# Two deformable-sampling layers: padded image through DRAM, third window buffer, second patch-sum bank, columns made on TensorE, filler matmuls between the layers

## The reference

```python
# layer 0: 4 sampled points per pixel, softmax weights, 1x1 projection, batch norm, gelu
offsets = conv2d(bev, offset_w, offset_b)              # 3x3, 8 channels out
attn = softmax(conv2d(bev, weight_w, weight_b), axis=1) # 3x3, 4 channels out
sampled = grid_sample_border(bev, gx, gy)              # bilinear, 4 corners per point
aggregated = einsum('bkhwd,bkhw->bdhw', sampled, attn)
y = conv2d(aggregated, proj_w); y = batchnorm(y); return gelu(y)

# layer 1: deformable 3x3 convolution, 9 sampled points per pixel, sigmoid gates
offset = conv2d(x, w_p, b_p); m = sigmoid(conv2d(x, w_m, b_m))
x_off = g_lt*x[lt] + g_rb*x[rb] + g_lb*x[lb] + g_rt*x[rt]   # bilinear
return conv2d(x_off * m, w_conv, stride=3)
```

## Time and profile before

| | us |
|---|---|
| three runs | 570.9, 572.35, 576.16 (median 572.35) |
| profiled execution, its own time | 566.8 |
| span of the profile, first to last instruction | 564.9 |
| TensorE busy (matmul) | 471.1 (83%) |
| VectorE busy | 391.0 (69%) |
| ScalarE busy | 147.2 (26%) |
| GpSimd busy | 345.4 (61%), of it 320 gathers 331.8 |
| mean granted clock of TensorE | 0.905 of full |

### The profile page before, as it was taken

One profiled execution on the slowest core, in us unless ns is written; L12 is line 12 of the kernel. 1 busy time (PEld: TensorE's weight loads), 2 busy tenths in 40 slices (PEclk: granted clock), 3 DMA queues, 4 the chain that ended last, 5 costly groups with the idle time before them and its releaser, 6 DMA issues.

```text
span 564.9 us, 10597 instructions
## 1 busy us (share of the span) xinstructions
PE 471.1 (83%) x3808; PEld 261.8 (46%) x3808; DVE 391.0 (69%) x874; ACT 147.2 (26%) x290; POOL 345.4 (61%) x335
## 2 busy tenths in 40 slices
PE   6679648879695480899999999899999999998894
PEld 3345335555453440354555555355544544543443
DVE  1627527587764650788898797798888788787671
ACT  2311111021102460234333433332332232332201
POOL 4317716754700005677777777777777777777771
PEclk9655878998989585899999999999999999999987
DMA  4379964566850089812232233821212212211211
GB/s 108 114 212 200 207 162 99 122 126 115 153 110 4 19 236 155 185 47 70 74 91 70 69 86 91 108 57 54 59 49 57 56 55 57 57 52 51 57 52 27
DMA packets 50148, 53.28 MB, mean 94 GB/s; under 512 B 24990, under 2 KB 41622, under 8 KB 50096
## 3 DMA queue, kind: packets, MB, share of 16 engines
q1 hardware_dynamic: 39712, 31.28, 26.7%
q0 software_dynamic: 10240, 20.99, 14.0%
q10 hardware_dynamic: 144, 0.30, 0.2%
HBM read 35.85 MB, written 8.72 MB: 79 GB/s over the span
## 4 chain that ended last, share of the span: by engine, by line
PE 35%; POOL 22%; issue 15%; DMA 11%; SPq 7%; DVE 6%; ACT 1%; POOLq 1%; DVEq 0%; ACTq 0%
POOL got L599 22%; SPq L456 5%; PE ps_x L1009 5%; PE ps_pair L1144 4%; PE ps_later L1144 4%; PE ps_x L1157 3%; DMA shared<-positions 3%; PE ps_raw L944 3%; DMA got<-table,idx 2%; PE ps_raw L1120 2%; DMA xn<-xq 2%; DMA columns_of<-table 2%; PE ps_x L1167 2%; DVE samples L1766 2%; PE ps_pair L1019 1%
## 5 line engine op out<-in xcount | busy, mean ns | idle before, releaser
L599 POOL DMA_INDIRECT got<-table,idx x320 | 331.8, 1037 | 137.5 <-issue 95.5
L1766 DVE TENSOR_TENSOR samples<-shared,vprod 128x800 f32<-128x800 f32 x48 | 47.2, 986 | 32.0 <-PE ps_x L1009 20.3
L1009 PE MATMUL ps_x<-early,samples 128*128 128x128 f32 (+1 forms) x336 | 49.3, 296 | 23.8 <-ACT ysumT L705 14.9
L1584 DVE TENSOR_TENSOR vprod<-ps_pair,rhat 128x704 f32<-128x704 f32 x64 | 56.7, 886 | 17.0 <-PE ps_pair L1144 16.5
L1783 DVE TENSOR_TENSOR prod<-got,wgt 128x512 f32<-128x512 f32 x64 | 44.2, 690 | 33.3 <-DMA got<-table,idx 33.1
L1009 PEld LDWEIGHTS ps_x<-early,samples 128*128 128x128 f32 (+1 forms) x336 | 39.3, 145 | 44.9 <-ACT ysumT L705 21.1
L1584 DVE TENSOR_TENSOR vprod<-ps_later,rhat 128x704 f32<-128x704 f32 x64 | 56.3, 880 | 0.2 <-PE ps_later L1144 0.2
L1157 PE MATMUL ps_x<-early,vprod 128*128 128x128 f32 x384 | 55.6, 281 | 0.6 <-DVE vprod L1592 0.4
L1157 PEld LDWEIGHTS ps_x<-early,vprod 128*128 128x128 f32 x384 | 41.9, 143 | 29.8 <-issue 19.4
L1592 DVE TENSOR_TENSOR vprod<-vprod 128x640 f32<-128x640 f32 x64 | 52.7, 824 | 1.2
L1167 PE MATMUL ps_x<-early,prod 128*128 128x128 f32 x256 | 39.3, 276 | 9.3 <-DVE prod L1783 9.1
(11 more groups left out here) (202 smaller groups left out, 657.1 us busy)
## 6 DMA issues: line engine op xcount, KB each, us to landing
shared<-positions SPq DMA_DIRECT2D x24, 440.0 KB, 7.9
got<-table,idx POOLq DMA_INDIRECT x320, 5.4
xn<-xq SPq DMA_DIRECT2D x28, 132.0 KB, 3.0
xn<-xq SPq DMA_DIRECT2D x28, 131.9 KB, 3.1
table<-trow SPq DMA_DIRECT2D x3, 702.0 KB
table<-trow SPq DMA_DIRECT2D x9, 234.0 KB
table<-trow SPq DMA_DIRECT2D x2, 1024.0 KB, 5.5
columns_of<-table SPq DMA_DIRECT2D x4, 512.0 KB, 8.9
```

The source lines that it names most:

```text
L599: pool.indirect_dma_start(into[t][:, s * P:(s + 1) * P], None, tab, bass.IndirectOffsetOnAxis(ap=idx[:, slot, k:k + 1], axis=0),).then_inc ...
L1009: last = nc.tensor.matmul(window_bank[0:m, t * P:(t + 1) * P], wprod[t % 2][:, a:a + m], idn[:], start=(q == 0), stop=(q == len(cuts) - 1) ...
L1584: nc.vector.tensor_tensor(dst, ps_dense[pair_number(0, t, pair) % 2][:].rearrange("p (d n) -> p d n", d=2)[:, :, 0:WROWS * C].rearrange("p ...
L1766: nc.vector.tensor_tensor(wprod[t % 2].rearrange("p (y x c) -> p y x c", y=SIDE, c=C), window[n // TT % 2][:, :, 2 * t * C:(2 * t + SIDE) ...
```

## The change

- **The padded image goes through DRAM.** A normalised image is written once to `image` (DRAM, 68 rows of 66 a channel), and `xn` is loaded from there, two transfers a quarter in place of four. The borders of `image` are zeroed by eight small transfers at the start, so the memset of `xn[:, 1]` goes, and that of `xn[:, 0]` covers eleven rows only. The heads are eleven rows for the lower shifts, and a convolution waits for fewer quarters.
- **Order of the start.** Four input transfers in place of eight; TensorE's filler matmuls at the start (4 and 1) go; image 0 is normalised before its heads; the statistics of image 1 are combined ahead of the last two corner chunks; SyncE's queue has corners and pixels of image 0 ahead of its quarters 2 and 3, and three windows ahead of image 1.
- **Three window buffers** in place of two, and **two banks** for the window sums; `y_bank[3]` is now `ps_raw`, `pixel_bank` is one bank.
- **The flag** of the slow path is loaded before the last projections and statistics.
- **Between the layers**: `keep_busy(3)` twice. One filler is a 128x128 by 128x448 matmul (two instructions) into a bank that nothing reads.
- **Layer 1**: the table is sent as 4, 3 and 2 chunks, its last rows on ScalarE's queue; the columns of image 0 come from `make_columns` (four calls of eight matmuls of 64 columns by 128) and four copies (two on ScalarE, two on VectorE), not from DRAM.

```diff
-SENT = [range(a, a + 3) for a in range(0, PT, 3)]
+SENT = [range(0, 4), range(4, 7), range(7, PT)]
+IMAGE = (H + 4) * WP
+NWIN = 3
...
+        image = [[nc.dram_tensor(f"image{l}{b}", [C, IMAGE], F32, kind="Internal").ap() for b in range(B)] for l in range(2)]
...
-        window_bank = ps_x[1]
-
-        y_bank = [ps_x[2], ps_o, ps_tab[0], ps_tab[1]]
+        window_bank = [ps_x[1], ps_tab[1]]
+
+        y_bank = [ps_x[2], ps_o, ps_tab[0], ps_raw]
...
-            return [k for k in ((q, q + 1) if h else (q - 1, q)) if 0 <= k < Q]
+            return [k for k in ((q, q + 1) if h else (q,)) if k < Q]
...
+            def clear_borders(l, b):
+
+                sp.dma_start(image[l][b][:, 0:WP], zero[0:C, 0:WP]).then_inc(borders_out, 16)
+                sp.dma_start(image[l][b][:, (H + 1) * WP:IMAGE], zero[0:C, :]).then_inc(borders_out, 16)
+
+            def send_image(l, b):
+
+                sp.dma_start(bass.AP(image[l][b].tensor, WP, [[QFLAT, Q], [IMAGE, C], [1, QFLAT]]),
+                             xq[:, b, WP:WP + QFLAT]).then_inc(image_out[b], 16)
+
+            def load_shifted(l, b, q, skip=0):
+
+                sp.wait_ge(image_out[b], 16 * (l + 1))
+                a, z = (q * QROWS + skip) * WP, ((q + 1) * QROWS + (2 if q == Q - 1 else 0)) * WP
+                for dy in range(2):
+                    sp.dma_start(xn[2 * C * dy:2 * C * (dy + 1), b, a:z],
+                                 bass.AP(image[l][b].tensor, a + dy * WP, [[1, 2], [IMAGE, C], [1, z - a]])).then_inc(xn_in[b][q], 16)
...
-                if n >= 2:
-                    sp.wait_ge(win_used, TT * (n - 1))
+                if n >= NWIN:
+                    sp.wait_ge(win_used, TT * (n + 1 - NWIN))
...
-            sp.wait_ge(pads_zero, PADS["xn0"])
+            for l in range(2):
+                for b in range(B):
+                    clear_borders(l, b)
+            sp.wait_ge(borders_out, 16 * 4 * B)
             sp.wait_ge(norm_xq, 1)
-            for q in range(Q):
-                load_shifted(0, q, 0 if q else HEAD)
-                if q % 2:
-                    send_corners(0, HALVES[q // 2], tab_copied, tab_out["00"])
+            send_image(0, 0)
+            send_corners(0, HALVES[0], tab_copied, tab_out["00"])
+            load_shifted(0, 0, 0, HEAD + 1)
+            load_shifted(0, 0, 1)
+            send_corners(0, HALVES[1], tab_copied, tab_out["00"])
             send_pixels(0)
+            load_shifted(0, 0, 2)
+            load_shifted(0, 0, 3)
+            sp.dma_start(later_sb[:], later).then_inc(later_in, 16)
             sp.wait_ge(margin_out, 64)
             sp.wait_ge(tab_out["positions0"], 16)
-            load_window(0)
-            load_window(1)
-            sp.dma_start(later_sb[:], later).then_inc(later_in, 16)
-            sp.wait_ge(pads_zero, PADS["xn1"])
+            for n in range(NWIN):
+                load_window(n)
             sp.wait_ge(norm_xq, 2)
+            send_image(0, 1)
             for q in range(Q):
-                load_shifted(1, q)
+                load_shifted(0, 1, q)
+            send_pixels(1)
...
             sp.wait_ge(norm_xq, 3)
-            load_shifted(0, 0, HEAD)
-            load_shifted(0, 1)
+            send_image(1, 0)
             for k, ts in enumerate(SENT):
-                if k == 1:
-                    load_shifted(0, 2)
-                    load_shifted(0, 3)
                 sp.wait_ge(tab_copied, NT + ts.stop)
                 send_rows(table[1][0], ts, tab_out["10"])
-            send_last_rows(table[1][0], tab_out["10"])
-            load_columns(0)
+                if k == 0:
+                    load_shifted(1, 0, 0, HEAD + 1)
+                    load_shifted(1, 0, 1)
+            load_shifted(1, 0, 2)
+            load_shifted(1, 0, 3)
...
-            nc.gpsimd.memset(xn[:, 0, :], 0.0).then_inc(pads_zero, 1)
+            nc.gpsimd.memset(xn[:, 0, 0:(HEAD + 1) * WP], 0.0).then_inc(pads_zero, 1)
             pool.wait_ge(pads_zero, PADS["power"])
             invert(1, 0)
-            nc.gpsimd.memset(xn[:, 1, :], 0.0).then_inc(pads_zero, 1)
...
+            act.wait_ge(tab_copied, NT + PT)
+            for ap, rows in last_rows(table[1][0]):
+                act.dma_start(ap, rows).then_inc(tab_out["10"], 16)
+            for k in range(2):
+                copy_columns(k)
...
+            def make_columns(k):
+
+                pe.wait_ge(tab_copied, NT + PT)
+                for r in range(TT):
+                    a = (1 + TT * k + r) * WP + 1
+                    for h in range(2):
+                        last = nc.tensor.matmul(table_bank[k][W * h:W * (h + 1), r * P:(r + 1) * P], xq[:, 0, a:a + W],
+                                                idn[:], start=True, stop=True)
+                last.then_inc(columns_mm, 1)
...
-                if t == 0 and i >= 1:
-                    pe.wait_ge(ysumT_copied[1], i)
+                if t == 0 and i >= 2:
+                    pe.wait_ge(ysumT_copied[1], i - 1)
...
-            keep_busy(4)
-            pe.wait_ge(x_in[0], 16 * Q)
+            pe.wait_ge(x_in[0], 32)
             pe.wait_ge(ends_zero, 2)
             make_corners(0, range(0, 2), tab_copied, tab_mm)
             combine(1, 0, 2, first_stats)
             make_corners(0, range(2, 4), tab_copied, tab_mm)
-            keep_busy(1)
             start_conv0(0)
             make_corners(0, range(4, 6), tab_copied, tab_mm)
             turn_item(ITEMS[0])
+            pe.wait_ge(variance, 1)
+            combine(2, 2, 4, first_stats)
             make_corners(0, range(6, PT0), tab_copied, tab_mm)
             start_conv0(1)
             start_conv0(2)
             turn_item(ITEMS[1])
-            pe.wait_ge(variance, 1)
-            combine(2, 2, 4, first_stats)
...
+            flag = is_far(pe)
             fold_y(1, len(WGROUPS) - 1)
             fold_y(0, NGA - 1)
-            with pe.If(is_far(pe)):
+            with pe.If(flag):
...
             combine(3, 0, 2 * B, later_stats)
+            keep_busy(3)
             pe.wait_ge(variance, 3)
             turn_edge(0)
             combine(4, 0, 2, later_stats)
+            keep_busy(3)
             pe.wait_ge(norm_xq, 3)
...
             make_rows(0, CHUNKS[EARLY_ROWS:], NT, tab_copied, tab_mm)
+            for k in range(TT):
+                make_columns(k)
             end_conv1(0)
...
+            normalise(0, 0)
             head(0, 0)
-            normalise(0, 0)
...
+            flag = is_far(dve)
             for j in (3, 0):
                 y_statistics(j)
-            with dve.If(is_far(dve)):
+            with dve.If(flag):
...
             row_weights(0)
+            for k in range(2, TT):
+                copy_columns(k)
```

More of the change, by code:

```diff
@@ L220, in build @@
         ysumT = sb("ysumT", [P, 2, GPIX])
-        shared = sb("shared", [P, (TT + 2) * WIN * C])
+        shared = sb("shared", [P, NWIN * SIDE * WLONG])
         window = [shared[:, k * SIDE * WLONG:(k + 1) * SIDE * WLONG].rearrange("p (y n) -> p y n", y=SIDE)
-                  for k in range(2)]
+                  for k in range(NWIN)]
         sampT = shared[:, 0:9 * GPIX].rearrange("p (s n) -> p s n", s=9)
@@ L260, in build @@
         x_in = [sem(f"x_in{b}") for b in range(B)]
+        image_out = [sem(f"image_out{b}") for b in range(B)]
+        borders_out = sem("borders_out")
         xn_in = [[sem(f"xn_in{b}{q}") for q in range(Q)] for b in range(B)]
@@ L291, in build @@
         used = sem("used")
-        win_in = [sem(f"win_in{k}") for k in range(2)]
+        win_in = [sem(f"win_in{k}") for k in range(NWIN)]
         win_used = sem("win_used")
@@ L426, in build @@
         ROWS_IN = {1: [0], 2: [1, 2], 3: [3, 4], 4: [5, 6], 5: [7, 8]}
-        PADS = {name: n + 1 for n, name in enumerate(("zero", "power", "xq", "xn0", "xn1"))}
+        PADS = {name: n + 1 for n, name in enumerate(("zero", "power", "xq", "xn0"))}
         EARLY_ROWS = 7
@@ L685, in copy_corners, with copy_conv @@
                                          ACT.Copy).then_inc(copied, 1)
-            def copy_conv(l, n, k, made, copied, n_turned=None, n_spread=None, N=None):
+            def copy_conv(l, n, k, made, copied, n_turned=None, n_spread=None, N=None, bank=ps_raw):
                 N = N or CONV1
@@ L764, in _ @@
                 for n in range(len(AGAIN)):
-                    copy_conv(0, n, 0, again["conv_raw"], again["conv_sb"], N=12)
+                    copy_conv(0, n, 0, again["conv_raw"], again["conv_sb"], N=12, bank=again_conv)
                     exps(0, n, again["logit"], again["gate"])
@@ L925, in turn_edge, with convolve @@
                                  raw[:, b, QPIX - W:QPIX], start=True, stop=True).then_inc(edge_mm, 1)
-            def convolve(l, b, r, made, blocks=range(4)):
+            def convolve(l, b, r, made, bank=ps_raw):
                 N = 3 * S_OF[l]
                 v = xn[:, b, :].rearrange("p (r c) -> p r c", c=WP)
-                for k in blocks:
+                for k in range(4):
```

(14 more changed lines are left out.)

107 lines of the change are left out of this document (60 added, 47 removed).

## The result

The changed kernel takes 628.01 us (median of 4 runs, 625.75 to 634.51) against 573.19 for the kernel before, run beside it: a ratio of 1.097, 95% interval 1.089 to 1.106. Forecast were 546 us, and a range of 533 to 560. The profiled run took 634.51 us, its span is 632.4.

What follows compares the result with a forecast made beforehand. Four stages with different limits: a start-up chain, TensorE in layer 0, a serial chain between layers, GpSimd's gathers in layer 1. Gains 2 + 16 + 1.5 + 6.5 = 26 us off 566.8 gave 540.8, scaled to 546; range 533 to 560.

Steps and rivals of the forecast that it cites:

- the price of the image: Start: `xn` needs two transfers in series through DRAM, 2.7 us beside 1 MB of corners (5.3 us), 3 to 8 in all.
- Rival D: Start and layer 0: transfers bind with 2 MB more before 76 us; gain 14 us, 558 us; chance 0.09.
- Start: 2 us: Up to the first product: `xq` ready 6.4 us earlier, less the image's transfers; gain 2 us, bounds -6 and +5.
- The term for the memset: Start: the removed memset had slowed VectorE's two heads beside it; 3.2 us, bounds 0 and 3.45.
- Layer 0: 16 us of 22.6: Layer 0: removed waits 19.6 us plus 3 for the clock, of which 70% is gained; bounds 8 and 23.
- the 12.4 for the third buffer: Layer 0: the third window's late arrival goes, 8.2 us, and the later window waits, 4.2 us.
- the 5.3 for the bank: Layer 0: a second bank removes TensorE's waits for ScalarE's copy of the sums, 6.7 us less about 1.4.
- the other 4.9, the shifted image 1 and the clock: Layer 0: 1.9 us of the 2.9 waited for shifted image 1, and 3 us from half clock after long waits.
- Flag and fillers: 1.5: Between the layers: earlier flag load 1 us (0 to 2.5), fillers holding the clock +0.5 us (-1.8 to +2.4).
- Layer 1's start: First gather 4.1 us earlier, columns 7.4 earlier, so the 2.39 us wait goes; gain 6.5 us, bounds +9 and -4.
- Rival E: Layer 0: TensorE at half clock for good; over a share of 0.4 it costs 36 us: 582 us; chance 0.06.
- the late window: Layer 0, sign of a wrong prediction: the third window still comes late, as behind the 8.23 us wait before.

Runs made afterwards that it cites:

- all_wide: The changed kernel with image writes, `xn` loads and input loads cut into transfers with 32 channels outermost: 539.59 us, ratio 0.942 to the kernel before.
- image_16_16: all_wide with each 32-channel image write cut into 16 and 16 channels: 542.51 us, ratio 0.950 to the kernel before.

## Why the prediction was wrong

The step that failed is the price of the image: "The image is 540 KB; the nearest rate is 198 GB/s, so 2.7 us ..., 3 to 8 us in all." It is a rate of all 16 engines, given to a transfer that used 4. The loads into `xn` were not priced at all, only counted: "eight issues replace sixteen". They used 2. The 4 and the 2 are what the packets show: the image landed after 10.75, 16.5 and 12.8 us in the chain, and the narrow loads into `xn` alone cost 67 us. Rival D, the transfers bind, had the right place, but priced it by bytes, with the engines 90% busy: 558 us, 12 over the forecast, where 82 over it were measured, with the transfer engines 45 to 63% idle in the two stretches of the start. I had read the bytes and the place in the queue of each transfer, and not its access pattern.

With that one thing mended, in all_wide or image_16_16, the other steps can be read off:

- *Start: 2 us.* Measured 3.0 and 0.5. `xq` is normalised at 11.64 in all_wide, 6.9 us earlier than before (18.59), 6.4 forecast. The term for the memset was right: without it beside them the two heads take 1.23 us, where they took 4.44, 3.2 forecast. The third convolution runs at 30.9 and 33.5, 31 to 35 forecast.
- *Layer 0: 16 us of 22.6.* Measured 18.0 and 18.4, 80% of the sum and not 70%. Two of its parts were undone one by one: the 12.4 for the third buffer gave 12.2, the 5.3 for the bank 4.5. For the other 4.9, the shifted image 1 and the clock, 1.7 us are left.
- *Flag and fillers: 1.5.* From the last projection to the first transposes it was 16.1 us and is 15.7, with or without the fillers. The fillers give 0, then, and TensorE's wait of 3.70 us in the earlier trace rows, at which the flag was aimed, is 3.1 in all_wide and 3.4 in image_16_16; no run takes the flag back alone. The second three took 4.20 us in all_wide and 2.50 in image_16_16, and either way the transposes came 15.6 to 15.7 us after the last projection. That the moment of the clock's change varies is what "TensorE: Matmul & The Clock Gate" of the Trainium skill, weighed in the prediction, says in its section "What's actually happening"; here it changed nothing.
- *Layer 1's start: 4.1 earlier and the wait of 2.39 gone.* From the transposes to the first gather, 20.7 before, it is 16.7 and 18.1: 4.0 and 2.6. The wait is gone. `make_columns` takes 1.97 + 1.92 us for its 64 instructions, 5 were forecast. The fixed cost of about 2.0 us that the prediction takes from the Trainium skill is given there for transfers issued by GpSimd; these image writes are SyncE's, and the 132 KB ones of all_wide landed after 1.9 to 2.4 us.
- *Sum: 26 us.* By the last gather, 552.63 before, it is 524.50 and 529.00: 28.1 and 23.6. In time: 539.6 and 542.5 us, where 546 was forecast for the kernel with the transfers as I had priced them.

Rival E, half clock for good, was put at 582 and slower. That it alone had the sign right is luck, for the mechanism was not there: the granted clock was 0.82 in 151:178, where it was 0.87 before.

Of what was to show it wrong, the late window came true: VectorE waited 15.6 us for windows in layer 0, 13.7 of them at once. So did the third convolution, named for 35 us at the latest: the second runs at 46.61 and the third at 63.12.

## What to carry to other kernels

Price a transfer by the engines that it uses, not by its bytes alone: read its two access patterns, and if either begins with a count that has no large divisor up to 16 (2, 4 and 17 here), cut it into several transfers whose outermost dimension is a multiple of 16 (16 and 32 here). In a profile the sign is compute engines waiting behind a transfer while the DMA share is low, and issues in the queue of several us each. Merging transfers saves about 0.4 us of issuing for each one that goes; here it cost 88.

## What the hardware showed beyond that

- Slow transfers hold up the queue behind them: single issues took 8.26 and 8.49 us in the change and at most 2.87 in all_wide up to the second image. The 8.49 is that of a window, whose own pattern begins with 64; what held it up is not shown.
- A cut of 32 channels into 17 and 15 costs 26 us over 16 and 16, in the write of the image alone.
- Transfers over few engines do not spread out beside each other: two with an outermost 2 took 15.70 us together, longer than the single one over 4 (10.75), and only two packets were under way at once.
- A GpSimd memset of 128x4356 values slowed VectorE's work beside it: two operations on 32x640 took 4.44 us with it and 1.23 without.
- Matmuls whose results fill 64 of the 128 columns, in turn the lower and the upper half, took 1.97 us for 32, 0.06 us each, where seven full ones take 0.95 us, 0.14 each. Whether the two halves overlap, or each is shorter by itself, no run separates.
- Without fillers TensorE was granted half clock (1.2 GHz) in 170:175 and 0.71 of full in 175:180; with them (image_16_16) 0.91 and 1.00. So the fillers did bring back the full 2.4 GHz earlier, and it was worth nothing, since the transposes waited for `xq` from VectorE in any case.
